# Cross-attention with image tokens: x's scale found apart from the context's, late loads on SP, ACT's table first, and another bank for the transposed Gram parts

## The chip, the cores and the metric

The kernel runs on one core of a Trainium2 chip. The metric is device time in microseconds (us). PE is TensorE, DVE VectorE, ACT ScalarE, POOL GpSimd, and SP issues most of the DMAs.

## The reference

For each of 8 batches, x (512 x 320) attends with 20 heads of 16 to 508 text tokens of 512 columns and, apart from them, to 4 image tokens. The image scores get half the cosine between each image token and the head's mean of the text tokens added.

```
q, k_t, v_t = heads(x @ W_q), heads(text @ W_k), heads(text @ W_v)
probs_t = softmax(q k_t^T * Dh**-0.5);  text_out = probs_t v_t
k_ip, v_ip = heads(ip @ W_k_ip), heads(ip @ W_v_ip)
qsem = l2norm(probs_t @ text);  sem = qsem @ l2norm(ip)^T
probs_ip = softmax(q k_ip^T * Dh**-0.5 + 0.5 * sem) * spatial_mask
out = (text_out + probs_ip v_ip) @ W_out + b_out + x
```

## The kernel before

The norm of qsem comes from a Gram matrix of the text tokens (text text^T) per batch, so that the kernel works in three stages: it prepares all 8 batches (q, k, v and Gram parts, stored to device memory), then runs attention over 640 units of 128 rows of one head, and then the image softmax and the output projection. The change lies in the first stage.

Matmuls of the first stage take fp16 operands split in two parts (hi, rest), which needs a scale for each operand: the largest absolute value bounds the split. DVE takes maxima over the columns of x and ctx (`column_sums`, L925 and L927) or squares of a weight (`weight_squares`, L966), sums their squares into a column of `sums`, PE spreads the sum over all partitions with a matmul by ones (`spread_sums`, L1247), DVE reads it into `top` (`find_top`, L935), ACT takes the root into `bound` and DVE the reciprocals into `scale` or `w_scale`. Then ACT writes an operand's hi part (L701 for weights, L692 for x, L695 for ctx) and DVE its rest (L980; L953 and L955; L960).

At the start, one spread (FIRST_JOB) serves ctx, x and W_q together, a second (W_JOB) W_k and W_v. PE's program is: spread, spread, Q of batch 0, K, spread for batch 1, image tokens (L1254 to L1270), V, image scores, Gram. ACT issues fourteen loads before its first operation: the three weights, W_out in two parts, the mask and b_out eight times. SP loads x and ctx of batch 0, the image tokens and their weights, and then batch 1's columns once both rests of batch 0 are done.

PE's program of each batch: Q in 3 tiles (24 matmuls, L1285, banks 0 to 2), K in 3 tiles (36, banks 3 to 5), V in 4 (48, banks 6, 0, 1, 2), scores of the image tokens (24 fp32 matmuls of 80 columns, L1342, bank 7), Gram products in 4 tiles (48, banks 3 to 6), and six transposes that fill in the other side of the Gram matrix (L1360), which ACT copies out in three instructions (L800). Each tile has a job, a pair of a bank and the number of its use in the batch; `use` gives the count that the semaphores `bank_filled` and `bank_drained` of that bank reach with it, and PE waits before a job until the bank's use before it is drained:

```
USES = [3, 2, 2, 2, 2, 2, 2, 2]
Q_JOB = [(0, 1), (1, 1), (2, 1)]
V_JOB = [(6, 1), (0, 2), (1, 2), (2, 2)]
G_JOB, GT_JOB = [(3, 2), (4, 2), (5, 2), (6, 2)], (0, 3)
```

At the end of the stage SP stores the last K parts, issues the first loads of the attention stage, and then stores the last v_parts, which ACT waits for.

Of the kernel before, what the change touches and what calls it, by code (L numbers as in the profile page):

```python
# [5 lines left out]
def xattn_kernel(  # L6
# [31 lines left out]
    fp32 = mybir.dt.float32  # L38
    fp16 = mybir.dt.float16
    bf16 = mybir.dt.bfloat16  # L40
    ALU = mybir.AluOpType
# [52 lines left out]
    with stack:  # L94
        def sb(name, shape, dt):
            return stack.enter_context(nc.sbuf_tensor(name, shape, dt))

        def sem(name):
            return stack.enter_context(nc.semaphore(name))
# [53 lines left out]
        sums = sb("sums", [P, 5], fp32)  # L153
        top = sb("top", [P, 5], fp32)
        bound = sb("bound", [P, 5], fp32)
        w_scale = sb("w_scale", [P, 3], fp32)
        w_bound = sb("w_bound", [P, 2], fp32)
        ip_stat = sb("ip_stat", [ALLIP, 8], fp32)
# [62 lines left out]
        w_sums_ready = sem("w_sums_ready")  # L221
        stat_step = sem("stat_step")
        top_root_ready = sem("top_root_ready")
        w_root_ready = sem("w_root_ready")
        w_scale_ready = sem("w_scale_ready")
        scale_ready = sem("scale_ready")
# [62 lines left out]

        FIRST_USES = [0, 0, 0, 0, 0, 0, 0, 2]
        IP_USES, IP_AFTER = [1, 1, 1, 1, 0, 0, 0, 0], 1
        USES = [3, 2, 2, 2, 2, 2, 2, 2]
        R1 = 3
        FIRST_JOB, W_JOB = (7, -1), (7, 0)
        SCALE_JOB = (7, 1)
        Q_JOB = [(0, 1), (1, 1), (2, 1)]
        K_JOB = [(3, 1), (4, 1), (5, 1)]
        V_JOB = [(6, 1), (0, 2), (1, 2), (2, 2)]  # L300
        IPS_JOB = (7, 2)
        G_JOB, GT_JOB = [(3, 2), (4, 2), (5, 2), (6, 2)], (0, 3)

        def use(job, b):
            j, n = job
            if isinstance(b, int) and b == 0:
                return FIRST_USES[j] + n + (IP_USES[j] if n > IP_AFTER else 0)
            return FIRST_USES[j] + IP_USES[j] + USES[j] * b + n

# [88 lines left out]
        def load_values(eng, b, i, n):  # L398
            eng.dma_start(v_ring[:, n].rearrange("p h k c -> p h (k c)"),
                          v_parts[b, bass.ds(i * GROUP, GROUP), :, :].rearrange("h p c -> p h c")).then_inc(values_loaded[n], 16)  # L400

        @block.sync
        def _(sp):
# [36 lines left out]
            def first_heads():  # L440

                sp.wait_ge(in_lo_split, 2 * B)
                sp.wait_ge(parts_saved, 1 + 16 * 2 * NC * (B - 1))
                sp.wait_ge(v_saved, 1 + 16 * (B - 1))
                sp.wait_ge(u_saved, 1 + 16 * (B - 1))
                load_group(sp, 0, 0, 0)
                load_values(sp, 0, 0, 0)
                sp.dma_start(u_sb[:, 0, :], u_parts[0]).then_inc(u_loaded, 16)
                load_group(sp, 0, 1, 1)
                load_values(sp, 0, 1, 1)  # L450

            columns_of(1)
            store_batch(0, lambda: columns_of(2))
# [216 lines left out]
        def _(act):  # L670
            act.dma_start(wq_raw, w_q).then_inc(wq_loaded, 16)
            act.dma_start(wk_raw, w_k.rearrange("(e p) c -> p e c", p=P)).then_inc(wk_loaded, 16)
            act.dma_start(wv_raw, w_v.rearrange("(e p) c -> p e c", p=P)).then_inc(wv_loaded, 16)
            act.dma_start(wout[:, 0:2, :], w_out[0:2 * P, :].rearrange("(m p) c -> p m c", p=P)).then_inc(wout_loaded, 16)
            act.dma_start(wout[0:CT[2][1], 2, :], w_out[2 * P:C, :]).then_inc(wout_loaded, 16)
            act.dma_start(mask_col[:, :], spatial_mask.rearrange("(s p) -> p s", p=P), allow_slow_non_contiguous=True).then_inc(late_loaded, 16)
            for b in range(B):
                act.dma_start(vw[HIP:HIP + 1, b, :], b_out.rearrange("(a c) -> a c", a=1)).then_inc(late_loaded, 16)

            def scale_root(b):  # L680

                if isinstance(b, int) and b == 0:
                    act.wait_ge(bank_drained[FIRST_JOB[0]], use(FIRST_JOB, 0))
                    nc.scalar.activation(bound[:, 0:3], top[:, 0:3], ACT.Sqrt, scale=IN_TOP ** -2).then_inc(top_root_ready, 1)
                else:
                    act.wait_ge(bank_drained[SCALE_JOB[0]], use(SCALE_JOB, b - 1))
                    nc.scalar.activation(bound[:, 0:2], top[:, 0:2], ACT.Sqrt, scale=IN_TOP ** -2).then_inc(top_root_ready, 1)

            def split_x(b, par):

                act.wait_ge(scale_ready, b + 1)
                nc.scalar.activation(x_t[par][:, 0], raw_x, ACT.Identity, scale=scale[:, par, X_COL:X_COL + 1]).then_inc(in_hi_split, 1)  # L692

            def split_ctx(b, par):
                nc.scalar.activation(ctx_t[par][:, 0], raw_ctx, ACT.Identity, scale=scale[:, par, CTX_COL:CTX_COL + 1])\  # L695
                  .then_inc(in_hi_split, 1)

            scale_root(0)

            def weight_first(w, raw, n):  # L700
                nc.scalar.activation(w[:, 0, :, 0:C], raw, ACT.Identity, scale=w_scale[:, n:n + 1]).then_inc(w_hi_split, 1)  # L701
# [1 line left out]
            act.wait_ge(w_scale_ready, 1)  # L703
            weight_first(wq, wq_raw, WQ_COL)
            split_x(0, 0)
            act.wait_ge(bank_drained[W_JOB[0]], use(W_JOB, 0))
            nc.scalar.activation(bound[:, 3:5], top[:, 3:5], ACT.Sqrt, scale=IN_TOP ** -2).then_inc(w_root_ready, 1)
            split_ctx(0, 0)
            act.wait_ge(w_scale_ready, 5)
            weight_first(wk, wk_raw, WK_COL)  # L710
            act.wait_ge(ip_step, 1)
# [207 lines left out]

        @block.vector  # L920
        def _(dve):
            def column_sums(b):

                dve.wait_ge(x_loaded, 16 * (b + 1))
                nc.vector.tensor_reduce(col_max[:, ET:IN_TILES], raw_x, AX.X, ALU.max, apply_absolute_value=True).then_inc(stat_step, 1)  # L925
                dve.wait_ge(ctx_loaded, 16 * (b + 1))
                nc.vector.tensor_reduce(col_max[:, 0:ET], raw_ctx, AX.X, ALU.max, apply_absolute_value=True).then_inc(stat_step, 1)  # L927
                dve.wait_ge(stat_step, 2 * (b + 1))
                for col, (c0, c1) in ((CTX_COL, (0, ET)), (X_COL, (ET, IN_TILES))):
                    nc.vector.scalar_tensor_tensor(col_squares[:, c0:c1], col_max[:, c0:c1], 1.0, col_max[:, c0:c1], ALU.mult,  # L930
                                                   ALU.mult, accum_out=sums[:, col:col + 1]).then_inc(sums_ready, 1)

            def find_top(job, b, c0, c1):
                dve.wait_ge(bank_filled[job[0]], use(job, b))
                nc.vector.tensor_scalar(top[:, c0:c1], bank[job[0]][:, 0:c1 - c0], TINY, None, ALU.max)                  .then_inc(bank_drained[job[0]], 1)  # L935

            def make_scales(b, par):
                dve.wait_ge(top_root_ready, b + 1)
                nc.vector.reciprocal(scale[:, par, CTX_COL:X_COL + 1], bound[:, CTX_COL:X_COL + 1])
                nc.vector.reciprocal(kept_scale[:, b, 1:2], bound[:, CTX_COL:CTX_COL + 1])  # L940
                if not isinstance(b, int) or b > 0:
                    key_scale(b, par)
                nc.vector.tensor_scalar(scale[:, par, Q_COL:Q_COL + 1], bound[:, 2:3], bound[:, X_COL:X_COL + 1], None, ALU.mult)                  .then_inc(scale_ready, 1)

            def key_scale(b, par):
                nc.vector.tensor_scalar(kept_scale[:, b, 0:1], w_bound[:, 1:2], bound[:, CTX_COL:CTX_COL + 1], None, ALU.mult)
# [20 lines left out]
                                               accum_out=sums[:, col:col + 1]).then_inc(w_sums_ready, 1)  # L967

            weight_squares(WQ_COL, wq_raw, wq_loaded)
            column_sums(0)  # L970
            find_top(FIRST_JOB, 0, 0, 3)
            weight_squares(WK_COL, wk_raw, wk_loaded)
            weight_squares(WV_COL, wv_raw, wv_loaded)
            make_scales(0, 0)
            nc.vector.reciprocal(w_scale[:, WQ_COL:WQ_COL + 1], bound[:, 2:3]).then_inc(w_scale_ready, 1)

            def weight_rest(w, raw_w, col, order):

# [1 line left out]
                nc.vector.scalar_tensor_tensor(w[:, 1, :, 0:C], raw_w, w_scale[:, col:col + 1], w[:, 0, :, 0:C], ALU.mult,  # L980
                                               ALU.subtract).then_inc(w_split, 1)

            find_top(W_JOB, 0, 3, 5)
            weight_rest(wq, wq_raw, WQ_COL, 1)
            split_x(0, 0)
            dve.wait_ge(w_root_ready, 1)
            nc.vector.reciprocal(w_scale[:, 0:2], bound[:, 3:5]).then_inc(w_scale_ready, 1)
            nc.vector.tensor_scalar(w_bound[:, 0:1], bound[:, 3:4], SCALE, None, ALU.mult).then_inc(w_scale_ready, 1)
# [255 lines left out]
        def _(pe):  # L1244
# [30 lines left out]
            def batch(b, par, first, last_batch):  # L1275
# [13 lines left out]

                if first:  # L1290
                    pe.wait_ge(ones_made, 1)
                    pe.wait_ge(sums_ready, 2)
                    pe.wait_ge(w_sums_ready, 1)
                    spread_sums(FIRST_JOB, 0, 3)
                    pe.wait_ge(w_sums_ready, 3)
                    pe.wait_ge(bank_drained[W_JOB[0]], use(W_JOB, 0) - 1)
                    spread_sums(W_JOB, 3, 5)
                    pe.wait_ge(w_split, 1)
                pe.wait_ge(in_lo_split, 2 * b + 1)
                for m, (c0, cn) in enumerate(CT):  # L1300
                    j = Q_JOB[m]
                    free(j)
                    third = [(wq[:, 0, NC - 1, c0:c0 + cn], x_b[:, 0, NC - 1, :]),
                             (wq[0:64, 1, NC - 1, c0:c0 + cn], x_b[0:64, 0, NC - 1, :])]
                    products(bank[j[0]][0:cn, 0:S],
                             [(lambda a, c=c: wq[:, a, c, c0:c0 + cn], lambda a, c=c: x_b[:, a, c, :]) for c in range(NC - 1)],
                             third).then_inc(bank_filled[j[0]], 1)

                if first:
                    pe.wait_ge(w_split, 2)  # L1310
# [226 lines left out]
```

## Time and profile before

| | us |
|---|---|
| median of 3 runs | 1746.62 (1746.57 to 1747.4) |
| profiled execution | 1759.38 |
| its span | 1757.7 |
| PE busy in it | 1684.9 |

In the rows below, a timeline or chain row begins with the start and the duration in us; a bracket at its end holds the idle time of the engine before it and what ended that. An xN counts the instructions that a row puts together, whose records overlap a little. A row of windows has the stretch, its length, the busy time and the number of instructions of each engine shown (PE, its weight loads, then DVE, ACT and POOL where all are shown), the granted clock of PE (1.00 is 2.4 GHz, 0.50 is 1.2 GHz), the DMA engines' share and their GB/s.

### The profile page before, as it was taken

The page shows a single profiled execution, that of the slowest core. Times are in us where ns is not written, and L with a number is a line of the kernel's source. Part 1 is how long each engine was busy: PE and PEld are TensorE (multiplying, and loading weights), DVE is VectorE, ACT ScalarE, POOL GpSimd, SP SyncE. Part 2 cuts the span into 40 slices and gives each one's busy share as a digit, 9 for nine tenths or more (in the row PEclk, how much of TensorE's full clock was granted, in tenths as well). Part 3 has the DMA queues.
Part 4 walks back from the last instruction along what each step waited for, and adds up shares of the span by engine and source line. Part 5 has one row for each costly group of instructions (what it writes and reads, how often), then busy time and mean ns, then how long its engine had stood idle before and what let it go on. Part 6 is the DMA issues. An engine that isn't in the chain of part 4 may idle for free.

```text
span 1757.7 us, 48715 instructions
## 1 busy us (share of the span) xinstructions
PE 1684.9 (96%) x13898; PEld 1048.6 (60%) x13898; DVE 1306.6 (74%) x2982; ACT 1156.2 (66%) x2604; POOL 1237.1 (70%) x1157
## 2 busy tenths in 40 slices
PE   4999999799999999998999999989999999999999
PEld 2766676466666666665666666656666666666465
DVE  6454542578888888886888888868888888888784
ACT  3455553677777777776777777767777777777321
POOL 4232333688888888887888888878888888888320
PEclk9899998899999999999999999999999999999999
DMA  5457656766666557664665665556557655664132
GB/s 203 127 131 184 166 147 153 122 102 110 107 124 107 105 100 128 117 111 84 132 116 107 111 118 105 105 114 106 101 107 126 100 106 115 117 113 82 43 113 96
DMA packets 490736, 204.94 MB, mean 117 GB/s; under 512 B 454296, under 2 KB 480224, under 8 KB 490624
## 3 DMA queue, kind: packets, MB, share of 16 engines
q1 hardware_dynamic: 488528, 201.18, 57.4%
q10 hardware_dynamic: 2096, 2.22, 0.4%
q8 instruction: 75, 1.23, 0.3%
q14 instruction: 37, 0.30, 0.1%
HBM read 68.27 MB, written 34.39 MB: 58 GB/s over the span
## 4 chain that ended last, share of the span: by engine, by line
PE 84%; DVE 6%; issue 5%; DMA 2%; ACT 1%; DVEq 1%; SPq 1%; POOL 0%; ACTq 0%; POOLq 0%
PE bank L1416 29%; PE bank L1417 18%; PE bank L1285 10%; PE bank L1381 7%; PE bank L1390 6%; PE bank L1481 3%; PE bank L1415 3%; PE bank L1421 3%; PE bank L1482 1%; PE bank L1342 1%; DVE neg_max L1104 1%; DVE probs L1113 1%; DVE late L1119 1%; DMA reduced<-in_L_xattn_W_v 1%; DMA v_parts<-v_sb 1%
## 5 line engine op out<-in xcount | busy, mean ns | idle before, releaser
L1416 PE MATMUL bank<-u_sb,late 127*128 127x508 f16 x2560 | 945.6, 375 | 0.0
L1417 PE MATMUL bank<-u_sb,late 127*128 127x508 f16 (+3 forms) x2560 | 762.5, 298 | 0.0
L1104 DVE TENSOR_REDUCE neg_max<-bank 128x1 f32<-128x508 f32 x640 | 437.5, 684 | 254.5 <-PE bank L1381 250.2
L611 POOL TENSOR_TENSOR wkv<-probs,wkv 128x508 f16<-128x508 f32 x384 | 432.6, 1127 | 202.8 <-ACT wkv L837 202.8
L1415 PE MATMUL bank<-v_ring,late 127*128 127x41 f16 x2560 | 468.8, 183 | 12.0 <-DVE probs L1113 11.9
L1113 DVE SCALAR_TENSOR_TENSOR probs<-bank,probs 128x508 f32<-128x508 f32 x640 | 432.0, 675 | 7.1 <-PE bank L1417 7.1
L618 POOL TENSOR_TENSOR probs<-probs,wkv 128x508 f32<-128x508 f32 x384 | 428.2, 1115 | 0.0
L1415 PEld LDWEIGHTS bank<-v_ring,late 127*128 127x128 f16 x2560 | 246.8, 96 | 255.1 <-issue 29.1
L1416 PEld LDWEIGHTS bank<-u_sb,late 127*128 127x128 f16 x2560 | 248.6, 97 | 167.8 <-issue 2.5
L625 POOL TENSOR_TENSOR probs<-probs,v_sb 128x508 f32<-128x508 f32 x256 | 294.7, 1151 | 0.0
L817 ACT ACTIVATE exp_bias<-neg_max 128x1 f32<-128x1 f32 x384 | 77.9, 203 | 298.0 <-DVE neg_max L1104 298.0
L1381 PE MATMUL bank<-raw 96*128 96x508 bf16 x640 | 241.9, 378 | 22.4 <-issue 11.6
L828 ACT ACTIVATE probs<-bank,exp_bias 128x508 f32<-128x508 f32 x384 | 257.2, 670 | 0.0
L837 ACT ACTIVATE wkv<-probs 128x508 f16<-128x508 f32 x384 | 240.6, 627 | 22.3 <-ACT probs L828 8.0
L1417 PEld LDWEIGHTS bank<-u_sb,late 127*128 127x128 f16 x2560 | 244.8, 96 | 0.0
L828 ACT ACTIVATE probs<-bank,neg_max 128x508 f32<-128x508 f32 x256 | 174.3, 681 | 14.8 <-DVE neg_max L1104 14.8
L1421 PEld LDWEIGHTS bank<-v_ring,late 127*128 127x128 f16 x2560 | 130.3, 96 | 75.6 <-issue 0.5
L1119 DVE SCALAR_TENSOR_TENSOR late<-bank,late 127x512 f16<-127x512 f32 x256 | 175.1, 684 | 0.0
L1421 PE MATMUL bank<-v_ring,late 127*128 127x41 f16 x2560 | 165.8, 181 | 0.0
L578 POOL TENSOR_TENSOR late<-work,late 128x512 bf16<-128x512 f32 (+3 forms) x48 | 55.1, 1151 | 155.7 <-ACT late L741 155.7
L1390 PEld LDWEIGHTS bank<-ident,probs 128*127 128x127 f32 x1024 | 153.7, 190 | 7.0
L844 ACT ACTIVATE v_sb<-probs 128x508 f16<-128x508 f32 x256 | 156.3, 611 | 0.0
(150 smaller groups left out, 1801.3 us busy)
## 6 DMA issues: line engine op xcount, KB each, us to landing
raw<-k_parts SPq DMA_DIRECT2D x192, 79.4 KB, 3.5
raw<-in_ctx_cols SPq DMA_DIRECT2D x8, 1016.0 KB, 7.5
raw<-q_parts SPq DMA_DIRECT2D x32, 240.0 KB, 3.5
u_parts<-u_sb SPq DMA_DIRECT2D x8, 825.5 KB, 8.3
u_sb<-u_parts SPq DMA_DIRECT2D x8, 825.5 KB, 5.3
v_parts<-v_sb SPq DMA_DIRECT2D x8, 820.0 KB, 13.2
v_ring<-v_parts SPq DMA_DIRECT2D x32, 205.0 KB, 3.8
raw<-in_x_cols SPq DMA_DIRECT2D x8, 768.0 KB, 4.5
```

What stands on the lines that cost most here:

```text
L611: nc.gpsimd.tensor_tensor(rows[:, 1, :, 0:TP], probs[:, j % PROB_RING, :].rearrange("p (k t) -> p k t", k=TT), rows[:, 0, :, 0:TP], ALU.su ...
L618: nc.gpsimd.tensor_tensor(own, own, flat_rows(j)[:, 1, :, 0:TP], ALU.add).then_inc(turned_weight_ready, 1)
L625: nc.gpsimd.tensor_tensor(own, own, half_hi[:, slot_of(j), :], ALU.subtract).then_inc(plain_weight_ready, 1)
L828: nc.scalar.activation(probs[:, j % PROB_RING, :], bank[S_BANK + j % 2][:, 0:T], ACT.Exp, bias=bias[:, j % 4:j % 4 + 1]).then_inc(probs_re ...
L1104: nc.vector.tensor_reduce(neg_max[:, j % 4:j % 4 + 1], bank[S_BANK + j % 2][:, 0:T], AX.X, ALU.max, negate=True)\
L1113: nc.vector.scalar_tensor_tensor(own, bank[Y_BANK + j % 2][:, 0:T], 1.0 if is_turned(j) else 2.0 * PROB_SCALE, own, ALU.mult, ALU.mult, ac ...
L1381: nc.tensor.matmul(bank[S_BANK + j % 2][:, 0:T], q_ring[:, n, h, st * P:(st + 1) * P], k_ring[:, n, h, :], start=True, stop=True).then_inc ...
L1390: last = nc.tensor.transpose(bank[PT_BANK + pair_of(j)][0:TP, k * P:(k + 1) * P], probs[:, j % PROB_RING, k * TP:(k + 1) * TP], ident[:, :])
L1415: nc.tensor.matmul(o, hi_k, v_ring[0:TP, n, h, k, :], start=(k == 0), stop=False)
L1416: nc.tensor.matmul(y, hi_k, u_sb[0:TP, par, GH[k]:GH[k] + T], start=(k == 0), stop=False)
L1417: done = nc.tensor.matmul(y[:, k * TP:T], hi_k, u_sb[0:TP, par, UL[k]:UL[k] + U_COLS[k]], start=False, stop=(k == TT - 1))
L1421: done = nc.tensor.matmul(o, both[1][:, k, :], v_ring[0:TP, n, h, k, :], start=False, stop=(k == TT - 1))
```

## The change

x and W_q get a spread and a root of their own (X_JOB), ahead of ctx's (CTX_JOB); ctx's scale is made after W_q's rest. The spread for W_k and W_v (W_JOB) comes after Q's first tile on PE, and the squares of W_v after x's rest on DVE. W_out, the mask and b_out are issued by SP behind its own first loads. ACT does a root into an unused tile as its first operation. The transposed Gram parts (GT_JOB) go to bank 2, as its third use, where they went to bank 0.

```diff
-        FIRST_USES = [0, 0, 0, 0, 0, 0, 0, 2]
+        FIRST_USES = [0, 0, 0, 0, 0, 0, 0, 3]
-        USES = [3, 2, 2, 2, 2, 2, 2, 2]
+        USES = [2, 2, 3, 2, 2, 2, 2, 2]
-        FIRST_JOB, W_JOB = (7, -1), (7, 0)
+        X_JOB, CTX_JOB, W_JOB = (7, -2), (7, -1), (7, 0)
-        G_JOB, GT_JOB = [(3, 2), (4, 2), (5, 2), (6, 2)], (0, 3)
+        G_JOB, GT_JOB = [(3, 2), (4, 2), (5, 2), (6, 2)], (2, 3)
...
@@ SP, behind its first loads
+            sp.dma_start(wout[:, 0:2, :], w_out[0:2 * P, :].rearrange("(m p) c -> p m c", p=P)).then_inc(wout_loaded, 16)
+            sp.dma_start(wout[0:CT[2][1], 2, :], w_out[2 * P:C, :]).then_inc(wout_loaded, 16)
+            sp.dma_start(mask_col[:, :], spatial_mask.rearrange("(s p) -> p s", p=P), allow_slow_non_contiguous=True).then_inc(late_loaded, 16)
+            for b in range(B):
+                sp.dma_start(vw[HIP:HIP + 1, b, :], b_out.rearrange("(a c) -> a c", a=1)).then_inc(late_loaded, 16)
...
@@ ACT (the same four statements are taken out of it)
+            act.wait_ge(ones_made, 1)
+            nc.scalar.activation(unused[:, :], ones[:, 0:1], ACT.Sqrt).then_inc(table_loaded, 1)
...
-            scale_root(0)
+            act.wait_ge(bank_drained[X_JOB[0]], use(X_JOB, 0))
+            nc.scalar.activation(bound[:, 1:3], top[:, 1:3], ACT.Sqrt, scale=IN_TOP ** -2).then_inc(x_root_ready, 1)
...
             act.wait_ge(w_scale_ready, 1)
             weight_first(wq, wq_raw, WQ_COL)
             split_x(0, 0)
+            act.wait_ge(bank_drained[CTX_JOB[0]], use(CTX_JOB, 0))
+            nc.scalar.activation(bound[:, 0:1], top[:, 0:1], ACT.Sqrt, scale=IN_TOP ** -2).then_inc(top_root_ready, 1)
+            act.wait_ge(scale_ready, 1)
+            split_ctx(0, 0)
             act.wait_ge(bank_drained[W_JOB[0]], use(W_JOB, 0))
             nc.scalar.activation(bound[:, 3:5], top[:, 3:5], ACT.Sqrt, scale=IN_TOP ** -2).then_inc(w_root_ready, 1)
-            split_ctx(0, 0)
...
@@ DVE
             weight_squares(WQ_COL, wq_raw, wq_loaded)
-            column_sums(0)
-            find_top(FIRST_JOB, 0, 0, 3)
+            x_maxima(0)
+            dve.wait_ge(stat_step, 1)
+            sum_squares(X_COL, ET, IN_TILES)
+            ctx_maxima(0)
+            dve.wait_ge(stat_step, 2)
+            sum_squares(CTX_COL, 0, ET)
+            find_top(X_JOB, 0, 1, 3)
+            dve.wait_ge(x_root_ready, 1)
+            nc.vector.reciprocal(w_scale[:, WQ_COL:WQ_COL + 1], bound[:, 2:3]).then_inc(w_scale_ready, 1)
+            nc.vector.reciprocal(scale[:, 0, X_COL:X_COL + 1], bound[:, X_COL:X_COL + 1]).then_inc(x_scale_ready, 1)
+            find_top(CTX_JOB, 0, 0, 1)
+            nc.vector.tensor_scalar(scale[:, 0, Q_COL:Q_COL + 1], bound[:, 2:3], bound[:, X_COL:X_COL + 1], None, ALU.mult)
             weight_squares(WK_COL, wk_raw, wk_loaded)
-            weight_squares(WV_COL, wv_raw, wv_loaded)
-            make_scales(0, 0)
-            nc.vector.reciprocal(w_scale[:, WQ_COL:WQ_COL + 1], bound[:, 2:3]).then_inc(w_scale_ready, 1)
...
+            weight_rest(wq, wq_raw, WQ_COL, 1)
+            dve.wait_ge(top_root_ready, 1)
+            nc.vector.reciprocal(kept_scale[:, 0, 1:2], bound[:, CTX_COL:CTX_COL + 1])
+            nc.vector.reciprocal(scale[:, 0, CTX_COL:CTX_COL + 1], bound[:, CTX_COL:CTX_COL + 1]).then_inc(scale_ready, 1)
+            split_x(0, 0)
+            weight_squares(WV_COL, wv_raw, wv_loaded)
             find_top(W_JOB, 0, 3, 5)
-            weight_rest(wq, wq_raw, WQ_COL, 1)
-            split_x(0, 0)
...
@@ PE
-                    pe.wait_ge(sums_ready, 2)
-                    pe.wait_ge(w_sums_ready, 1)
-                    spread_sums(FIRST_JOB, 0, 3)
-                    pe.wait_ge(w_sums_ready, 3)
-                    pe.wait_ge(bank_drained[W_JOB[0]], use(W_JOB, 0) - 1)
-                    spread_sums(W_JOB, 3, 5)
+                    pe.wait_ge(sums_ready, 1)
+                    pe.wait_ge(w_sums_ready, 1)
+                    spread_sums(X_JOB, 1, 3)
+                    pe.wait_ge(sums_ready, 2)
+                    pe.wait_ge(bank_drained[CTX_JOB[0]], use(CTX_JOB, 0) - 1)
+                    spread_sums(CTX_JOB, 0, 1)
...
+                    if first and m == 0:
+                        pe.wait_ge(w_sums_ready, 3)
+                        pe.wait_ge(bank_drained[W_JOB[0]], use(W_JOB, 0) - 1)
+                        spread_sums(W_JOB, 3, 5)
```

## Rows read from the trace of the kernel before

**Rows 1.** The page of the whole execution: busy time of the engines.
```profile
PE 1684.9 (96%) x13898; PEld 1048.6 (60%) x13898; DVE 1306.6 (74%) x2982; ACT 1156.2 (66%) x2604; POOL 1237.1 (70%) x1157
```

**Rows 2.** List of waits, PE, 60 to 312: in total, times, longest.
```profile
PE bank L1285 <- ACT u_sb L800: 7.3, 7, 1.1
```

**Rows 3.** The chain that ended last: start, us, what.
```profile
61.27 6.67 PE bank L1285 x48
...
90.19 3.71 PE bank L1342 x24
93.90 8.35 PE bank L1285 x48
...
124.45 3.71 PE bank L1342 x24
...
303.55 12.98 DMA v_parts<-v_sb
```

**Rows 4.** Timeline of PE: start, duration, instructions, idle time before.
```profile
17.90 0.58 PE L1247 MATMUL bank<-sums,ones 128*128 128x2 f32 x2 [4.66 <-DVE late L966]
...
136.34 0.52 PE L1360 MATMUL bank<-ident,u_sb 127*127 127x127 f16 x6
137.88 5.90 PE L1285 MATMUL bank<-reduced,wq 128*128 128x512 f16 x24 [1.02 <-ACT u_sb L800]
```

**Rows 5.** Timeline of ACT.
```profile
13.14 1.28 ACT L684 ACT_TABLE_LOAD   x1 [13.14 <-issue]
14.44 0.20 ACT L684 ACTIVATE bound<-top 128x3 f32<-128x3 f32 x1
...
18.20 1.09 ACT L701 ACTIVATE wq<-probs,w_scale 128x960 f16<-128x960 f32 x1 [3.56 <-DVE w_scale L975]
...
136.90 0.93 ACT L800 ACTIVATE u_sb<-bank 127x127 f16<-127x127 f16 x3
```

**Rows 6.** Windows of batch 0's and batch 1's Gram products, all engines.
```profile
61.20:67.90 6.70, 6.70 (x51) 5.47 (x51) 3.44 (x5) 2.73 (x7) 2.98 (x2) 1.00 0.55 165
...
94.10:97.50 3.40, 3.40 (x10) 1.84 (x9) 1.79 (x1) 0.44 (x1) 2.70 (x2) 0.50 0.15 33
```

**Rows 7.** Timeline of SP's queue.
```profile
25.87 0.35 SPq L407 DMA_DIRECT2D raw<-in_x_cols  x1
```

**Rows 8.** DMA issues from 0 to 26: size, time to landing.
```profile
probs<-in_L_xattn_W_k ACTq DMA_DIRECT2D x1, 640.0 KB, 11.4
reduced<-in_L_xattn_W_v ACTq DMA_DIRECT2D x1, 640.0 KB, 14.6
```

**Rows 9.** Timeline of DVE, the start.
```profile
8.09 1.75 DVE L925 TENSOR_REDUCE col_max<-raw 128x3 f32<-128x1536 f32 x1
9.96 2.27 DVE L927 TENSOR_REDUCE col_max<-raw 128x4 f32<-128x2032 f32 x1
...
16.35 1.49 DVE L966 SCALAR_TENSOR_TENSOR late<-reduced 128x1280 f32<-128x1280 f32 x1 [1.50 <-DMA reduced<-in_L_xattn_W_v]
...
18.53 0.16 DVE L935 TENSOR_SCALAR top<-bank 128x2 f32<-128x2 f32 x1 [0.36 <-PE bank L1247]
...
19.33 1.22 DVE L980 SCALAR_TENSOR_TENSOR wq<-probs,w_scale,wq 128x960 f16<-128x960 f32 x1 [0.64 <-ACT wq L701]
...
20.80 1.28 DVE L953 SCALAR_TENSOR_TENSOR reduced<-raw,scale,reduced 128x1024 f16<-128x1024 f32 x1 [0.25 <-ACT reduced L692]
...
22.88 0.17 DVE L987 RECIPROCAL w_scale<-bound 128x2 f32<-128x2 f32 x1
```

**Rows 10.** Windows of L1285 alone, the first Q and K products.
```profile
22.99:26.38 3.39, 3.39 (x9) 1.02 (x10) 1.00 0.00 0
...
30.20:38.30 8.10, 8.01 (x37) 3.48 (x36) 1.00 0.54 187
```

**Rows 11.** Windows of L1270 alone.
```profile
41.03:43.97 2.94, 2.94 (x25) 2.84 (x25) 0.82 0.74 237
43.97:48.51 4.54, 4.54 (x24) 4.34 (x24) 0.50 0.08 24
```

More of the change, by code:

```diff
@@ L155, in xattn_kernel @@
         bound = sb("bound", [P, 5], fp32)
+        unused = sb("unused", [P, 1], fp32)
         w_scale = sb("w_scale", [P, 3], fp32)
@@ L223, in xattn_kernel @@
         top_root_ready = sem("top_root_ready")
+        x_root_ready = sem("x_root_ready")
+        x_scale_ready = sem("x_scale_ready")
+        table_loaded = sem("table_loaded")
         w_root_ready = sem("w_root_ready")
@@ L673, in _, with split_x @@
             act.dma_start(wv_raw, w_v.rearrange("(e p) c -> p e c", p=P)).then_inc(wv_loaded, 16)
[L674 to L678, printed above, removed]
+            act.wait_ge(ones_made, 1)
+            nc.scalar.activation(unused[:, :], ones[:, 0:1], ACT.Sqrt).then_inc(table_loaded, 1)
             def scale_root(b):
+                act.wait_ge(bank_drained[SCALE_JOB[0]], use(SCALE_JOB, b - 1))
+                nc.scalar.activation(bound[:, 0:2], top[:, 0:2], ACT.Sqrt, scale=IN_TOP ** -2).then_inc(top_root_ready, 1)
+            def split_x(b, par):
                 if isinstance(b, int) and b == 0:
-                    act.wait_ge(bank_drained[FIRST_JOB[0]], use(FIRST_JOB, 0))
-                    nc.scalar.activation(bound[:, 0:3], top[:, 0:3], ACT.Sqrt, scale=IN_TOP ** -2).then_inc(top_root_ready, 1)
-                else:
[L686 to L691, printed above, removed]
+                    act.wait_ge(x_scale_ready, 1)
+                else:
+                    act.wait_ge(scale_ready, b + 1)
                 nc.scalar.activation(x_t[par][:, 0], raw_x, ACT.Identity, scale=scale[:, par, X_COL:X_COL + 1]).then_inc(in_hi_split, 1)
@@ L921, in _, with x_maxima, ctx_maxima, sum_squares @@
         def _(dve):
-            def column_sums(b):
+            def x_maxima(b):
                 dve.wait_ge(x_loaded, 16 * (b + 1))
                 nc.vector.tensor_reduce(col_max[:, ET:IN_TILES], raw_x, AX.X, ALU.max, apply_absolute_value=True).then_inc(stat_step, 1)
+            def ctx_maxima(b):
                 dve.wait_ge(ctx_loaded, 16 * (b + 1))
                 nc.vector.tensor_reduce(col_max[:, 0:ET], raw_ctx, AX.X, ALU.max, apply_absolute_value=True).then_inc(stat_step, 1)
+            def sum_squares(col, c0, c1):
+                nc.vector.scalar_tensor_tensor(col_squares[:, c0:c1], col_max[:, c0:c1], 1.0, col_max[:, c0:c1], ALU.mult,
+                                               ALU.mult, accum_out=sums[:, col:col + 1]).then_inc(sums_ready, 1)
+            def column_sums(b):
+                x_maxima(b)
+                ctx_maxima(b)
                 dve.wait_ge(stat_step, 2 * (b + 1))
-                for col, (c0, c1) in ((CTX_COL, (0, ET)), (X_COL, (ET, IN_TILES))):
-                    nc.vector.scalar_tensor_tensor(col_squares[:, c0:c1], col_max[:, c0:c1], 1.0, col_max[:, c0:c1], ALU.mult,
-                                                   ALU.mult, accum_out=sums[:, col:col + 1]).then_inc(sums_ready, 1)
+                sum_squares(CTX_COL, 0, ET)
+                sum_squares(X_COL, ET, IN_TILES)
             def find_top(job, b, c0, c1):
@@ L940, in make_scales @@
                 nc.vector.reciprocal(kept_scale[:, b, 1:2], bound[:, CTX_COL:CTX_COL + 1])
-                if not isinstance(b, int) or b > 0:
-                    key_scale(b, par)
-                nc.vector.tensor_scalar(scale[:, par, Q_COL:Q_COL + 1], bound[:, 2:3], bound[:, X_COL:X_COL + 1], None, ALU.mult)                  .then_inc(scale_ready, 1)
+                key_scale(b, par)
+                nc.vector.tensor_scalar(scale[:, par, Q_COL:Q_COL + 1], bound[:, 2:3], bound[:, X_COL:X_COL + 1], None, ALU.mult)\
+                  .then_inc(scale_ready, 1)
             def key_scale(b, par):
@@ L969, in _ @@
             weight_squares(WQ_COL, wq_raw, wq_loaded)
-            column_sums(0)
-            find_top(FIRST_JOB, 0, 0, 3)
+            x_maxima(0)
+            dve.wait_ge(stat_step, 1)
+            sum_squares(X_COL, ET, IN_TILES)
+            ctx_maxima(0)
+            dve.wait_ge(stat_step, 2)
+            sum_squares(CTX_COL, 0, ET)
+            find_top(X_JOB, 0, 1, 3)
[4 more added lines that the diff above has]
+            nc.vector.tensor_scalar(scale[:, 0, Q_COL:Q_COL + 1], bound[:, 2:3], bound[:, X_COL:X_COL + 1], None, ALU.mult)
             weight_squares(WK_COL, wk_raw, wk_loaded)
-            weight_squares(WV_COL, wv_raw, wv_loaded)
-            make_scales(0, 0)
-            nc.vector.reciprocal(w_scale[:, WQ_COL:WQ_COL + 1], bound[:, 2:3]).then_inc(w_scale_ready, 1)
             def weight_rest(w, raw_w, col, order):
```

## The prediction

> **What bounds the kernel now.** I read the page first: PE is busy for 96% of a span of 1757.7 us [rows 1], so time is won by letting PE start sooner, idle less, or run at its higher clock. Next the list of waits for the preparation of batches 1 to 7: it holds one wait of weight, PE's L1285 (the Q products) behind ACT's L800, 7 times, 7.3 us in all, the longest 1.1 [rows 2]. Then the chain that ended last. In this stage it runs over PE: projections, image scores (L1342), Gram products (L1285 x48), and at the stage's end it leaves PE, goes through the last K splits and SP's issues, and ends on the store of v_parts, which starts at 303.55 and lands 12.98 us later; the attention stage waits for it [rows 3]. That store is issued behind the last K splits, so what PE gains before the K products of batch 7 reaches the end. What PE gains after them (the eighth wait behind L800, after batch 7) does not. The attention stage, some 80% of the span, isn't touched. The sum is made against the profiled execution's 1759.38 us (span 1757.7); the timed runs have a median of 1746.62, 12.8 less. I carry the difference over unchanged.
>
> **The bank of the transposed Gram parts.** PE ends the six transposes at 136.86 and starts Q of the next batch at 137.88 [rows 4]: Q's first tile and the transposes share bank 0, which ACT's three L800 copies empty from 136.90 on, in 0.93 us [rows 5]. With the transposes in bank 2, Q's first two tiles run at once, on banks whose V products were drained long before. The wait passes to Q's third tile. Q's 24 matmuls fill 5.9 us [rows 4], so the third tile starts some 3.9 us after the first, 3 us behind the end of L800: nothing is left of the wait. Bank 2 was last used by the fourth V product, drained before the scores, so the transposes do not wait either. Each gap was 1.02 us, and neighbouring groups of matmuls overlap in the records by about 0.15, so each is worth 1.02 to 1.18; seven of them are 7.1 to 8.3, and I take **7.9 us**. ACT follows PE here: it, too, is simply asked sooner.
>
> **What this does to the clock.** Batch 0's 48 Gram matmuls take 6.67 us, batch 1's take 8.35 behind score matmuls of the same 3.71 us [rows 3]. The windows say why: batch 0 runs at a granted 1.00 (2.4 GHz), while 94.10 to 97.50 is at 0.50 (1.2 GHz) and gets 10 matmuls done [rows 6]. Each of batches 1 to 6 has such a drop, each time behind the small fp32 score matmuls, and each costs 8.35 - 6.67 = 1.68 us. But batch 0 does the same work without one, so whether it comes depends on how the scores lie in time. The batches lie alike now because all are about 34.26 long (scores at 90.19 and 124.45 [rows 3]). With one gap gone a batch is 33.1 with a drop and 31.4 without, so they will no longer lie alike and part of the drops should be missed. The trace cannot say how many. Bounds: none missed (0) and all six missed (10.1 us). I take the middle, three: **5.0 us**. The Trainium skill, "TensorE: Matmul & The Clock Gate", Part 1, says that the monitor behind this clock runs freely and does not restart with the kernel; if so, the number of drops would differ from run to run, and no run so far shows that.
>
> **The loads moved to SP.** ACT issues fourteen loads and comes to its first operation, the table load of 1.28 us, only at 13.14 [rows 5]. After the change the table is loaded by about 4 us. SP issues the eleven loads after its own five, and then has nothing to issue until 25.87, when batch 1's columns follow [rows 7]. Even if SP needed as long for the eleven as ACT for all fourteen, 13.1 us, it would be done near 17: hidden, and if that cover went (SP late by more than 4 us) batch 1's maxima on DVE would be next to wait. W_k and W_v land 11.4 and 14.6 us after their issue, at 12.7 and 16.3 [rows 8]; the moved loads stand behind them now and stand behind SP's own loads after, so I leave both where they are. The Trainium skill, "DMA: Bandwidth & Descriptors", Issuing engines are not separate DMA queues, says that another issuing engine saves only issue time; by it too the sum for the transfers would be nothing.
>
> **The split scales.** I lay the start out anew from the durations of [rows 9] and ACT's [rows 5]. DVE: W_q's squares end and x's maxima (1.75) start at 8.09 as now and end at 9.9, ctx's (2.27) to 12.5, then the top of x at 12.75. ACT's root takes 0.2, W_q's scale stands at 13.1, ACT's first part of W_q (1.09) ends at 14.3, and that of x well before DVE asks for it. DVE: W_k's squares (1.5) to 15.1, W_q's rest (1.22) to 16.4, two reciprocals, and x's rest, which now fills 20.80 to nearly 22.88, to 18.5. So PE starts Q at about 18.65 where it now starts at 22.99, 4.3 us sooner. But does that carry through? Three things say no. (1) The sums of W_k and W_v are spread only after Q's first tile, and that tile's 8 matmuls take 3.39 us [rows 10], about 0.43 each against 5.90 / 24 = 0.25 in a later batch [rows 4]. That is the pace of the lower clock, though the row prints 1.00; PE comes to them out of idle time before and after the change. They end at 22.05. The spread and its return to DVE take 0.63 (17.90 to 18.53 [rows 4, 9]), the top 0.16, the root 0.2: DVE makes W_k's scale at 23.0, against 22.88 now [rows 9]. (2) From there DVE's program is the old one, in the old order: ctx's rest, W_k's rest, image token norms, W_v's rest, residuals, batch 1's maxima. It was DVE and ACT, not PE, that this stretch ran on, and it ends where PE starts L1270 at 41.03 [rows 11]. (3) K's products then start near 27.3 in place of 30.20 and end near 35.4 in place of 38.3 [rows 10], so that PE only idles for 3 us more ahead of L1270. ACT's late root (14.44 [rows 5]) and DVE's wait for W_v are what was removed, and another wait of about 2 us (for the spread behind Q) took its place. Bounds of the start without the clock: 0.5 us gained (if W's spread slips in early) to 0.6 lost; I take 0.1 lost.
>
> The clock again: it falls at 42.9 now, so that the first 24 L1270 matmuls take 2.94 us at 0.82 and the other 24 take 4.54 at 0.50 [rows 11]. With PE idle from 35.4 it should fall up to 3 us sooner, and all of L1270 at the lower clock is 2 x 4.54 = 9.08: 1.6 us more. Bounds 0 and 2.5 (with some V products too); I take 1.2. The start thus costs **1.3 us**.
>
> **The sum.** 7.9 + 5.0 - 1.3 = 11.6 us less: 1747.8 for a profiled execution, and 1735.0 for the median.
>
> **The rivals.**
> Forecast, the gap goes and two to four drops are missed: 1746.6 - 7.9 + 1.3 = 1740.0, less 3.4 to 6.7, gives 1733 to 1737, and with the bounds of the start and the gaps 1731.5 to 1738.5. Chance 0.50.
> The drops stay in every batch: the scores are as long and as small as before, and six of six speak for it. Then it is the 1740.0 before the clock's part. Against it: batch 0. Chance 0.25.
> Nearly all drops go, or the earlier Q carries through as well: 1740.0 - 10.1 = 1730, or 1735 - 4.3 = 1731 with the latter. For it: PE is busy without a gap. Against: the points (1) to (3). Chance 0.12.
> The bank change does not do what it says, as another wait takes the gap's place, say Q's third tile behind L800 or the transposes behind a late drain of bank 2: gain of the clock alone or less, 1743 to 1748. The 3 us of slack speak against it. Chance 0.08.
> Slower: the low clock becomes longer in each batch. At the Gram products a drop of twice the length costs 1.7 us more; six batches give 10 and the start 1.3 to 3, against 7.9 won: 1746.6 - 7.9 + 10.1 + 2.5 = 1751. It decides once five of the batches double. For it: the change makes the timing drift; against: PE idles less, not more. Chance 0.05.
>
> **How the numbers follow.** Likeliest time 1735. The range runs from 1730 (nearly all drops gone) to 1741.5 (drops in every batch, gap at its lower bound): it holds the forecast, the rival with all drops and most of the third. 0.2% is 3.5 us, about what a measurement of this kernel can tell from no change. Faster by more holds the first three cases, 0.87; within it 0.08; slower 0.05.
>
> **What would show it.** PE's wait behind L800 gone from the list, batches 31.4 or 33.1 long with Gram products of 6.7 or 8.4; Q at about 18.7, K at 27.3, W_k's scale on DVE at 23.0 behind PE's spread, L1270 at about 41.1 with a granted 0.50 over all of it. The prediction is wrong if DVE makes W_k's scale well before 22.9, if L1270 starts before 40, or if the drops stay in all batches or vanish.

## The result and the profile after

The changed kernel takes 1741.04 us (median of 7 runs, 1735.53 to 1742.55), the kernel before beside it 1749.6 (7 runs, 1746.57 to 1756.76): ratio 0.9926, 95% interval 0.9906 to 0.9946, so 9 to 16 us less, about 13. The medians alone lie 8.6 us apart: three of the seven times of before are those that the prediction had (1746.57 to 1747.4), and the other four lie between 1749.6 and 1756.76, with a mean 12.7 us above that of the changed kernel. The kernel before spreads far wider than its first three runs let one see. The profiled execution of the changed kernel has a span of 1740.8 us, 16.9 below that of before.

The waits of PE from 55 to 312 us after the change, where [rows 2] had the seven behind ACT's copies of the transposed Gram parts (L810 in this kernel); the one that is left there is the last, after batch 7:

```profile
PE bank L1416 <- ACT probs L838: 11.0, 4, 8.9
PE bank L1416 <- ACT u_sb L810: 1.2, 1, 1.2
PE bank L1377 <- DVEq L1121: 0.7, 1, 0.7
```

The chain that ended last, to compare with [rows 3] (L1316 is L1285 of before, L1377 the image scores, L1395 the transposes, L1301 the image token products):

```profile
40.77 9.14 PE bank L1301 x48
49.91 8.05 PE bank L1316 x48
57.96 3.71 PE bank L1377 x24
61.67 6.67 PE bank L1316 x48
68.34 0.40 PE bank L1395 x6
68.74 13.67 PE bank L1316 x60
...
93.10 6.67 PE bank L1316 x48
99.77 0.35 PE bank L1395 x6
100.12 13.67 PE bank L1316 x60
...
124.63 8.16 PE bank L1316 x48
...
189.10 8.35 PE bank L1316 x48
...
291.02 12.12 DMA v_parts<-v_sb
```

From transposes to Q there is no gap, and from one Q to the next 31.38 us pass (68.74 to 100.12) where there is no drop. Of the Gram products of batches 1 to 6, those of batches 2, 4 and 6 meet the lower clock (a drop, from here on). The store of v_parts starts 12.53 us sooner than in [rows 3] and takes 0.86 us less. So 13.4 of the 16.9 us between the two spans come before the attention stage, and 3.5 in it.

The start, PE's timeline (compare [rows 4, 10]):

```profile
18.14 3.68 PE L1316 MATMUL bank<-reduced,wq 128*128 128x512 f16 x8 [5.08 <-DVE reduced L975]
21.75 0.39 PE L1278 MATMUL bank<-sums,ones 128*128 128x2 f32 x2
22.00 3.95 PE L1316 MATMUL bank<-reduced,wq 128*128 128x512 f16 x16
27.02 8.01 PE L1316 MATMUL bank<-reduced,wkv 128*128 128x508 f16 x36 [1.07 <-DVE wkv L1007]
38.25 0.35 PE L1278 MATMUL bank<-sums,ones 128*128 128x2 f32 x2 [3.21 <-DVE col_squares L943]
...
40.77 9.14 PE L1301 MATMUL bank<-reduced 128*128 128x32 f32 x48 [1.40 <-issue]
```

and DVE's (compare [rows 9]), which waits 2.65 us for the spread behind Q's first tile:

```profile
22.18 0.16 DVE L955 TENSOR_SCALAR top<-bank 128x2 f32<-128x2 f32 x1 [2.65 <-PE bank L1278]
22.62 0.17 DVE L1018 RECIPROCAL w_scale<-bound 128x2 f32<-128x2 f32 x1 [0.27 <-ACT bound L718]
```

Q starts 4.85 us sooner, W_k's scale is made 0.26 us sooner, and so are the image token products (40.77 for 41.03), which then run at the lower clock from the first to the last. The windows of these matmuls alone, columns as in [rows 11]:

```profile
40.77:45.30 4.53, 4.53 (x25) 4.40 (x25) 0.50 0.55 175
45.30:49.90 4.60, 4.60 (x25) 4.41 (x24) 0.50 0.01 2
```

One thing changed where the edit is not: PE's waits in the attention stage. Before:

```profile
PE bank L1415 <- DVE probs L1113: 11.9, 26, 0.7
PE bank L1381 <- issue: 11.6, 2, 6.0
```

After:

```profile
PE bank L1450 <- DVE probs L1144: 11.6, 25, 0.7
PE bank L1416 <- issue: 5.7, 2, 2.9
...
PE bank L1450 <- DMA late<-wkv: 1.5, 3, 0.5
```

The two waits in which PE waits for nothing that the profile shows fell from 6.0 and 5.6 to 2.9 and 2.8 us: 5.9 us that no step of the prediction speaks of.

### The profile page after: what moved, and what is told of

It is laid out like the page before. It is cut to its first block, busy times and chain, and to the rows that moved or that the text cites. A ratio compares the mean times of both kernels' runs of the same rounds, so it can differ in the third digit from the quotient of the medians.

```text
span 1740.8 us, 48742 instructions
## 1 busy us (share of the span) xinstructions
PE 1678.8 (96%) x13900; PEld 1046.5 (60%) x13900; DVE 1305.8 (75%) x2984; ACT 1157.5 (66%) x2606; POOL 1240.7 (71%) x1157
## 4 chain that ended last, share of the span: by engine, by line
PE 83%; DVE 6%; issue 5%; DMA 2%; SPq 2%; ACT 1%; DVEq 1%; POOL 0%; POOLq 0%; ACTq 0%
PE bank L1451 29%; PE bank L1452 18%; PE bank L1316 10%; PE bank L1416 7%; PE bank L1425 6%; PE bank L1516 3%; PE bank L1450 3%; PE bank L1456 3%; PE bank L1517 1%; PE bank L1377 1%; DMA late<-wkv 1%; DVE neg_max L1135 1%; DVE probs L1144 1%; DVE late L1150 1%; DMA v_parts<-v_sb 1%
## 5 line engine op out<-in xcount | busy, mean ns | idle before, releaser
L1450 PE MATMUL bank<-v_ring,late 127*128 127x41 f16 x2560 | 468.6, 183 | 13.2 <-DVE probs L1144 11.6
L1425 PE MATMUL bank<-ident,probs 128*127 128x128 f32 x1024 | 156.0, 274 | 0.0
```

Of the source, the lines that this page charges most:

```text
L1425: last = nc.tensor.transpose(bank[PT_BANK + pair_of(j)][0:TP, k * P:(k + 1) * P], probs[:, j % PROB_RING, k * TP:(k + 1) * TP], ident[:, :])
L1450: nc.tensor.matmul(o, hi_k, v_ring[0:TP, n, h, k, :], start=(k == 0), stop=False)
```

## The experiments

Ratios are to the kernel before on the same chip, whose single times lay between 1746.6 and 1762.0; they differ by up to 0.002 from the ratio of the medians. Runs one to four shared a chip, five to eight another, nine to twelve a third.

**One part alone.** The first kernel is before.py with two lines changed:

```diff
-        USES = [3, 2, 2, 2, 2, 2, 2, 2]
+        USES = [2, 2, 3, 2, 2, 2, 2, 2]
-        G_JOB, GT_JOB = [(3, 2), (4, 2), (5, 2), (6, 2)], (0, 3)
+        G_JOB, GT_JOB = [(3, 2), (4, 2), (5, 2), (6, 2)], (2, 3)
```

> The kernel before with the transposed Gram parts in bank 2 and nothing else changed. My theory: the seven waits of 1.02 to 1.11 us go (7.9 us) and about half of the six drops of PE's clock behind the image scores are missed (5.0 us more), while the start stays as it is: ratio to the kernel before 0.993 (0.991 to 0.996), with Q after the transposes without a wait and batches of 31.4 or 33.1 us. The rival, that the start's new order brings part of the gain: 0.996 or more here.

Measured: 1735.56 us, 0.9899 (0.9872 to 0.9926): below the expected range. One drop in batches 1 to 6, and waits at the restarts of the attention loop of 3.2 us at most. The second is the changed kernel with these two lines turned back:

> The changed kernel with the transposed Gram parts back in bank 0, so that only the new order of the start, the moved loads and the early table are left. My theory: a loss of 0 to 2 us by the clock of the L1270 stage (image tokens), which now runs at the lower clock from its beginning, and the drops come back in each of batches 1 to 6: ratio 1.000 (0.9985 to 1.0015). The rival, that Q's earlier start is worth its 4 to 5 us in the end: 0.9975.

Measured: 1749.83 us, 0.9978 (0.9958 to 0.9999), Q of batch 1 at 70.56. The drops did not come back in each batch, as was expected: the chain has them in batches 1 and 2 and none in batches 3 to 6, though the batches with a drop are 34.2 us long (Q at 70.56, 104.78, 138.99), about as in [rows 3].

```profile
95.30 8.11 PE bank L1316 x48
...
129.58 8.03 PE bank L1316 x48
...
163.52 6.67 PE bank L1316 x48
```

Neither theory had the ratio right for its reason: the restarts are short here too, 5.9 us in both together, so that a kernel with no gain or loss in the start would stand at 0.9967 or lower.

**What makes the drops.**

```diff
+        PAD = 5
...
                 last.then_inc(bank_filled[GT_JOB[0]], 1)
+                pe.wait_ge(bank_drained[IPS_JOB[0]], use(IPS_JOB, b))
+                for n in range(PAD):
+                    nc.tensor.matmul(bank[IPS_JOB[0]][0:TP, 0:T], ctx_b[:, 0, 0, 0:TP], ctx_b[:, 0, 0, 0:T], start=True, stop=True)
```

> The changed kernel with five extra matmuls of 508 columns behind the transposes of each batch (results unused, some 1.1 us), so that a batch takes about as long as it did before although PE has no idle time in it. My theory, that it is the length of a batch which decides how many drops of the clock there are: the batches lie alike again, a drop in five to seven of batches 1 to 7, and both parts of the gain are gone: ratio 0.999 to 1.001. The rival, that the idle time ahead of Q made the drops: three drops as in the changed kernel, only the 1.1 us per batch lost: ratio 0.9965 to 0.9975.

Measured: 1750.56 us, 0.9962 (0.9936 to 0.9987), but in two heaps: six of twelve times lie between 1739 and 1748, six between 1753 and 1756. The trace is of the upper heap (1755.70). Its chain shows a Gram stage at the lower clock in every batch from 1 on, 34.14 us apart, with no idle time in PE:

```profile
91.44 3.71 PE bank L1378 x24
95.15 8.35 PE bank L1317 x48
...
125.57 3.71 PE bank L1378 x24
129.28 8.35 PE bank L1317 x48
...
163.42 8.36 PE bank L1317 x48
...
197.56 8.36 PE bank L1317 x48
...
231.69 8.36 PE bank L1317 x48
```

So the idle time ahead of Q is not needed for the drops. By the ratio alone the rival's range (0.9965 to 0.9975) lies nearer; but both ranges took the restarts of the attention loop for unchanged, which are short here too (6.2 us in both), and it is the trace that decides, for its heap: drops without idle time. A batch of this length can meet a drop each time, but need not: the start alone had two in a row and then none (above). No trace of the lower heap was taken. The granted clock of each run, 0.983 to 0.989 in the lower heap and 0.980 or 0.981 in the upper, says that the lower one spent less time at 1.2 GHz.

> The kernel before, unchanged, for a second trace of it. By the trace of the first, five to seven of batches 1 to 7 have a drop of the clock; by the timed runs, which lie up to 15 us apart, the number could be anything. My theory, that a batch of 34.26 us keeps step with the drops once one has come: at least four in a row. The rival, that they fall at random: one to three, scattered. Q of batch 1 starts at 69.0 to 70.5 in both. PE's two waits of 6.0 and 5.6 us in the attention stage, 3 us each in the five later traces, tell whether those belong to the kernel before (6 again) or to that execution (3).

Measured: one execution, 1752.50 us, span 1750.8, the two waits at the restarts 11.5 us in all again, and a chain that keeps 32.57 us from Q to Q:

```profile
69.28 13.84 PE bank L1285 x60
...
90.10 3.71 PE bank L1342 x24
93.81 6.67 PE bank L1285 x48
101.85 13.84 PE bank L1285 x60
...
126.39 6.67 PE bank L1285 x48
134.43 13.84 PE bank L1285 x60
```

The same kernel, and no drop in batches 1 to 5; batch 6 has one. "At least four in a row" fell, and of the rival the number held, one. The six drops on which the prediction built were those of one execution. They count: here the attention stage starts at 311.22, 7.4 us sooner than in the first trace (318.62), with the same program.

**Scores between other matmuls.** The twelve score matmuls (24 in the records) are issued one after every second matmul of the fourth V product and of the first Gram product; V waits for `q_full`, `kip` and bank 7 ahead of its fourth tile. In the last batch DVE's step that frees bank 7 moves ahead of V.

```diff
+                def one_score(n):
+                    if n % 2 == 0:
+                        s, c = scores_of.pop(0)
+                        rn = CT[c][1]
+                        m = nc.tensor.matmul(bank[IPS_JOB[0]][:, s * HIP:(s + 1) * HIP], q_full[0:rn, c, s * P:(s + 1) * P],
+                                             kip_batch[0:rn, c, :], start=(c == 0), stop=(c == NC - 1))
```

> The changed kernel with the image scores' matmuls put one by one between the matmuls of the fourth V product and of the first Gram product (six each) rather than in a row. My theory, that a row of small fp32 matmuls is what lets the clock drop: no drop is left in batches 0 to 7 at this place, three times 1.68 us less than the changed kernel: ratio 0.990 to the kernel before, and batches of 31.4 us all. The rival, that fp32 matmuls count as little whatever stands between them, or that the mixture loses as much as it wins by switching weights: ratio 0.9926 or more.

Measured: 1734.3 us, 0.9888 (0.9861 to 0.9915): as expected, no drop between batches 0 and 7, and from Q to Q 31.0 or 31.3 us.

> The start of the kernel before, with the Gram parts in bank 2 and the image scores' matmuls between others: what is left if only the part that paid is kept. My theory: no drop in batches 1 to 6, the start 1.2 us better than with the changed order: 1 to 2 us less than the run with mixed scores and the changed start, ratio 0.988 to the kernel before. The rival, that the changed order of the start pays a little after all: equal or worse, 0.989 or more.

Measured: 1733.05 us, 0.9887 (0.9864 to 0.991), no drop. By the medians that is 1.3 us under the mixed scores with the changed start, which fits the theory; by the ratios the two are equal, which fits the rival: not decided. From the chain, Q to Q 31.04 us:

```profile
66.26 13.67 PE bank L1285 x60
79.92 0.31 PE bank L1247 x2
80.24 5.15 PE bank L1285 x37
...
97.30 13.67 PE bank L1285 x60
```

That is also 0.34 us less than the 31.38 of a batch without a drop in the changed kernel.

> The kernel before with the image scores' matmuls put between others, Gram parts still in bank 0: no drops, the seven gaps kept. The six drops of the first trace of before and the single one of the second say that their number is not fixed. If it is three on average (my guess now), this is 5 us under the kernel with the shifted instructions (given waits of 3 us at the restarts here too, which the trace will tell): ratio 0.9940 to the kernel before. The rival, that the kernel before has all six in most executions: 0.991.

Measured: 1740.87 us, 0.9929 (0.9904 to 0.9954), no drop, 5.7 us at the restarts: against the shifted kernel below (0.9957) 0.3% or about 5 us by the ratios and 2.8 us by the medians, with intervals that overlap.

**The start.** The spread for W_k and W_v inside Q's first tile:

```diff
+                def weights_spread(n):
+                    if n == 2:
+                        pe.wait_ge(w_sums_ready, 3)
+                        pe.wait_ge(bank_drained[W_JOB[0]], use(W_JOB, 0) - 1)
+                        spread_sums(W_JOB, 3, 5)
```

> The changed kernel with the spread for W_k and W_v after the third matmul of Q's first tile instead of after all eight. My theory, that the spread's place behind Q's tile is what takes the earlier Q's gain away: DVE makes W_k's scale at 20.6 in place of 22.6, and L1270's successor in the trace (image token products) starts at 38.8 in place of 40.8: 2 us less, ratio 0.9985 to the changed kernel, which is some 0.991 to the kernel before. The rival, that the path of the start is held elsewhere (x of batch 1, W_v, the clock): image token products at 40.8 as before and no gain.

Measured: 1740.25 us, 0.9924 (0.9901 to 0.9946). The mechanism is as expected, W_k's scale made at 20.80; PE's timeline:

```profile
18.30 1.44 PE L1316 MATMUL bank<-reduced,wq 128*128 128x512 f16 x3 [5.08 <-DVE reduced L975]
19.74 0.58 PE L1278 MATMUL bank<-sums,ones 128*128 128x2 f32 x2
...
38.95 9.13 PE L1301 MATMUL bank<-reduced 128*128 128x32 f32 x48 [1.55 <-issue]
```

The image token products start 1.82 us sooner than after the change. The gain in time, at most 2 us of 1740, can't be told from none. The changed kernel with mixed scores, this spread, and seventeen extra matmuls in PE's idle time ahead of the image token products:

> The changed kernel with mixed scores, with the spread inside Q's first tile, and with seventeen extra matmuls in PE's idle time of the start (twelve ahead of batch 1's spread, five ahead of the image token products, results unused) to keep its clock up. My theory: image token products at about 38.8, with the clock at 1.00 for the first part of them, so that they take 7.5 instead of 9.1 us: 3.5 us less than with mixed scores alone, ratio 0.987 to the kernel before. The rival, that the extra matmuls don't hold the clock or delay the stretch: 0.988 or more.

Measured: 1730.58 us, 0.9862 (0.9839 to 0.9884), the fastest of all. The image token products took 6.34 us in place of 9.14, but started at 40.83: the twelve extra matmuls ran until 38.9 and pushed batch 1's spread from 36.4 to 38.8. So they hold the clock and give back what the earlier spread had won.

**The restarts.** The kernel before with eight semaphore increments in PE's program ahead of the attention stage:

```diff
+            for _ in range(8):
+                apart(pe)
             for j in range(LEAD):
                 scores(0, j)
```

> The kernel before with eight semaphore increments that nothing waits for in PE's program ahead of the attention stage, so that the instructions of its loop stand eight places later; they run while PE idles. My theory, that the two waits of 6 us at the loop's restarts (3 us in every other kernel so far) come from where the loop's first instructions stand in the blocks of 16 KB in which instructions are loaded: two waits of 3 us and a ratio of 0.9967 to the kernel before. The rival, that they come from what else runs then: two waits of 6 us and 1.000.

Measured: 1743.63 us, 0.9957 (0.9934 to 0.9981), and two waits of 3.0 us. From the lists of waits of the shifted kernel (330 to 1734 us) and of the kernel before's second trace:

```profile
PE bank L1381 <- issue: 6.0, 2, 3.0
```

```profile
PE bank L1381 <- issue: 11.5, 2, 5.8
```

The instruction loads in the ten microseconds from such a restart on, first before (814 to 824), then shifted (804 to 814), from the DMA view (packets, MB, share):

```profile
q8 instruction: 3, 0.05, 2.3%
```

```profile
q8 instruction: 2, 0.03, 1.5%
```

Before, the loads begin at 814.5 and 817.7 and PE starts at 820.65, 3.0 us after the second; shifted, they begin at 804.6 and 807.7 and PE starts at 807.65, 3.1 us after the first. The clock follows: behind the wait it is 0.79 on average in 9.4 us before, and 1.00 shifted (windows):

```profile
820.60:830.00 9.40, 9.35 (x67) 5.08 (x68) 6.50 (x14) 5.05 (x13) 3.69 (x4) 0.79 0.14 26
```

```profile
807.60:817.00 9.40, 9.33 (x83) 5.70 (x84) 8.14 (x18) 6.67 (x17) 5.34 (x5) 1.00 0.16 30
```

That eight increments alone do this is shown. That the reason is the place of the loop's first instructions in a block is argued; for it speaks that every kernel whose program has another length has the short waits: the page counts 48715 instructions before, 48717 with mixed scores in it and 48721 with the bank change alone (waits of 3.2 us at most in both).

The twelve times fall in two heaps, seven from 1737.9 to 1744.5 and five from 1750.8 to 1754.3, some 12 us apart, about seven drops of 1.7. The trace is of the lowest time (1737.94) and has one drop in batches 1 to 6; that drops make the upper heap is not shown by a trace of it, but its granted clock is 0.980 to 0.983 and that of the lower heap 0.987 to 0.991.

**The change and its larger part once more, on one chip.**

> Gram parts in bank 2 alone, once more, beside the shifted kernel on the same chip. My theory now: of the 18 us that the first run of it showed, 7.9 are the seven gaps, 5.8 the restarts, and the rest drops and chance: 0.9918 to the kernel before, 8 to 10 us under the shifted kernel. The rival, that the drops of the kernel before stay with it and are the larger part: 12 us or more under the shifted kernel.

Measured: 1737.11 us, 0.9909 (0.9883 to 0.9935), 6.5 us under the shifted kernel by the medians, 8 by the ratios.

> The changed kernel once more, beside the bank change alone on the same chip. My theory: 1.2 us over the bank change alone, by the lower clock in the image token products of the start, and with chance in the drops between 0 and 4 us over it: ratio 0.9925 to the kernel before. The rival, that the new order of the start is no loss: equal.

Measured: 1741.14 us, 0.9931 (0.9907 to 0.9955), 4.0 us over the bank change alone; in the first round of runs it was 0.9926 against 0.9899, and the start alone against the shifted kernel is 0.9978 against 0.9957. These are three pairs with overlapping intervals, all with the same sign and near 4 us; the fourth, both with mixed scores, shows 1.3 us by the medians and nothing by the ratios (0.9888 against 0.9887). The new order of the start is a loss of some 1 to 4 us.

The traces say where. Up to the attention stage the pair with mixed scores, which has no drops, differs by 1.7 us (PE's first matmul behind the store of v_parts at 299.12 and 297.41). From there to the end the seven traces with the new start take 1433.2 to 1435.6 us and the five with the old start and short restarts 1426.9 to 1432.3; three of those five are of executions 4 to 6 us faster than their kernel's median, and the other two take 1431.4 and 1432.3. So a part of the loss, 1 us or more, lies in the attention stage, whose work the edit does not change.

## Why the prediction was right, and where it wasn't

The gain (11.6 us forecast, some 13 measured) came out, but two of the terms were wrong and made up for each other. The time (1735.0 forecast, 1730 to 1741.5) came out at 1741.0, half a microsecond inside the range, and that is luck: the forecast was taken off 1746.6, the median of three runs that agreed within 0.8 us, and the kernel before lies at 1753.8 to 1754.7 in the later rounds.

**The bank, 7.9 us: right.** The wait is gone from the list, nothing took its place, and Q to Q without a drop went from 32.57 us (second trace of before) to 31.38, 1.19 us; after some batches it is 0.2 to 0.3 us more. Over all seven, from the first Gram product of batch 0 to Q of batch 7, the second trace of before takes 205.4 us and the bank change alone 197.4, with one drop in each: 8.0 us. The bank change alone brings all of it, and more than the whole change.

**The clock between batches, 5.0 us: mis-sized, and its premise fell.** The traces of before and after show six and three drops, exactly the forecast. But "the batches lie alike now" held for one execution: the second has one drop in batches 1 to 6, and the times of the shifted kernel, with the same batches, make two heaps. With the change there are no two heaps 12 us apart: 13 runs of the changed kernel lie within some 7 us (1735.53 to 1742.55), with three drops in one trace and two in the other. The Trainium skill's statement that the monitor runs freely (TensorE: Matmul & The Clock Gate, Part 1), which the prediction set beside its sum, agrees with the two traces of before: six drops and one, by the same program. What the drops gave on average is the remainder, an estimate from the runs: 13 - 8.0 - 7.5 and the 1 to 4 us of the start added, so -1.5 to 1.5 us, which can't be told from nothing. That the drops need the row of small fp32 matmuls is shown by the four kernels without such a row: no drop in 24 batches (1 to 6 of each), of 31.0 to 31.3 or of 32.25 us, against 25 in the 60 batches of the ten traces with the row. It does not suffice: batch 0 has the same row and no drop in any trace.

**The start without the clock, 0.1 us lost: right to 0.4 us.** Q at 18.14 (18.65 forecast), W_k's scale at 22.62 (23.0), K at 27.02 (27.3), image token products at 40.77 (41.1). The earlier Q went nowhere, as its three reasons said, and the spread's place behind Q's tile was the first of them: inside the tile it let the products start 1.82 us sooner.

**The start's clock, 1.2 us: right where it was forecast, but not all.** The products took 9.14 us (9.08 forecast) in place of 7.48. But 7.48 was again one execution: with the old start these products took 8.4 us in the second trace of before and 8.0 in both of the bank change alone, so that the clock costs some 1 us here. In runs the start costs 1 to 4 us, where 1.3 was forecast. The loss at batch 1 in the traces is 0.5 to 1.8 us (Q at 68.74 and 69.81 against 68.28 and 67.99 with the bank change alone). Part of the rest is in the attention stage: waits for three late transposes, 1.3 to 1.9 us in all, in the changed kernel and in all but two of those made from it, and in none with the old start. The two without them (padded, and all together) take as long in that stage as the others, so these waits are not all of it. Whether the eleven loads moved into SP's program have a part in it was not tried; it stays open.

**The loads on SP: right.** SP's last issue of them ends at 13.8 us, and W_k and W_v land 11.3 and 14.4 us after their issue (11.4 and 14.6 before).

**What no step had: the restarts.** The prediction held the attention stage, 80% of the span, for untouched, and did not take up PE's two waits of 6 us in it. They shrink to 3 us with eight increments more in PE's program: 5.5 to 5.9 us of waits in the traces, 0.43% (0.19 to 0.66), about 7.5 us, in the runs. The clock that falls for less time, or not at all, behind a shorter wait (0.79 and 1.00 above) fits the difference. With the drops at nothing and the start at its 1 to 4 us, the prediction's own terms give 4 to 7 us; the rest is this one, which it put at nothing without reading these waits.

## What to carry to other kernels

When two jobs in a row share a PSUM bank, move the first to a bank that the jobs behind it need last: one wait per batch went for two changed constants. Put small matmuls between large ones before tuning around the clock's drops: it removed them, and with the old bank the times then lay within 5.7 us (6 runs) in place of 16.3 (12 runs). Take more than one trace before a sum is built on something that may fall otherwise in the next execution. And compare an edit with a kernel whose instructions are shifted but whose work is the same: here that alone was worth, by the best estimate, more than half of what the whole change brought.

## What the runs showed of the hardware that was not expected

- A loop of PE restarts after 3 or after 6 us, twice per execution, by eight instructions more or less ahead of it. Two loads of instructions start there, 3.2 us apart (814.5 and 817.7 before).
- The same program (the shifted kernel) on the same chip takes 1738 to 1744 or 1751 to 1754 us. Its batches are 32.6 us long without a drop of PE's clock and 34.3 with one; batches of that length met six drops in one trace, two in another and one in two more.
- PE's clock falls to 1.2 GHz although PE has no idle time, behind 3.7 us of small fp32 matmuls (padded, batches 1 to 6).
- Twelve small fp32 matmuls (24 in the records) between large fp16 ones cost 0.34 us less per batch than in a row, apart from the clock.
